# Mamba stage unrolled, with the recurrence of one batch beside the projections of the next

## The chip, the cores and the metric
The kernel is one program on one core of a Trainium2 chip. It runs eight stages one after the other (four attention-like and four feed-forward layers); the change is in the seventh, the Mamba layer. The metric is device microseconds of an execution. A core has TensorE (PE), VectorE (DVE), ScalarE (ACT), GpSimd (POOL) and SyncE (SP), each with its own instruction queue, which it works off in order; they wait for each other by semaphores. Matmuls write PSUM, which has eight banks of 128 x 512 fp32.

## The reference
Eight batches of 512 tokens with 256 channels go through all layers, each as `x + layernorm(layer(layernorm(x)))`. This is the Mamba layer, with 512 inner channels, 16 states, four taps and a step rank of 16:
```python
xr = x @ W_in.T
xc, res = (xr[..., :DI], xr[..., DI:])
u = depthwise_causal_conv(xc, W_conv)          # 4 taps a channel
u = silu(u + b_conv)
x_dbl = einsum('bdl,ed->ble', u, W_xproj)      # -> dt (16), B (16), C (16)
delta = softplus(dt @ W_dt.T + b_dt)
dA = exp(delta * A);  dBu = delta * B * u      # for each channel and state
h = dA_t * h + dBu_t                           # over the 512 tokens
y = sum_n(h * C) + u * D
out = (y * silu(res)) @ W_out.T
```

## The kernel before, in words
`stage_mamba` keeps channels on partitions: the 512 inner channels are four tiles (`ct`), tokens lie along the free dimension, 512 columns. After one block that loads weights and builds the selection table `sel`, a hardware loop `nc.Fori(0, NB)` runs the eight batches, one block each. Within a block the order of work is the order of the code of each engine:

- Projection: PE multiplies `w_in_t` with the normed, transposed rows (L1824), 8 tiles with K=256. ACT copies the first four to `xc` (L1779) and takes Silu of the others (`res`, L1781). VectorE convolves: four taps, 16 operations (L1704, L1707). ACT: Silu to `u_t` (L1785).
- PE projects `u_t` to 48 rows (L1829) and the step rows back to 512 channels (L1835). VectorE splits the B and C rows into three bf16 parts (L1716 to L1721), so that one bf16 matmul with `sel` can broadcast a row exactly over 128 partitions.
- Softplus: Abs, Exp, Ln on ACT (L1798, L1800, L1803), joined with a quadratic by three VectorE operations over all four tiles (L1729, L1731, L1732); then `delta` and `e_t = delta * u` (L1740).
- Recurrence: 64 units, state outside, tile inside. For each, ACT writes the decay exp(delta*A) to PSUM (L1812), VectorE makes dB (L1751) and scans over the tokens (L1762), POOL multiplies with the broadcast C (L1890), PE adds the product to the tile's sum in `pA` with an identity matmul (L1859). Per state, PE broadcasts C and B into the same bank (L1843, L1849) and ACT copies C out between them (L1795). Rings of three buffers.
- Norm of the next batch's rows is placed in the recurrence (L291 to L302, L138); output projection (L1873), then the output norm at the start of the next block (L151 to L179).

All eight PSUM banks are in use: `pA` four, `pX` two, `pY` two, which is at once decay and output.

## Time and profile before

| | |
|---|---|
| median of 3 runs | 6546.77 us (6545.3 to 6550.39) |
| profiled execution | 6538.69 us, span 6536.7 us |
| Mamba stage in the span | 4133.2 to 5577.6 us |
| busy over the span: PE, DVE, ACT, POOL | 68%, 47%, 29%, 29% |
| mean granted PE clock | 0.836 |

The busy shares are means over eight stages with different limits; the stage has to be read by itself. The granted clock is a share of 2.4 GHz, so 0.50 is the lower level, 1.2 GHz. In the timeline, a fp32 matmul of the code appears as two MATMUL instructions (two passes), and a group written "x4" has its start and its whole duration.

### The profile page before, as it was taken

To read this page: it belongs to the slowest core of one execution; us is meant where nothing else is said; L and a number is where in the kernel's file an instruction comes from. 1 tells how busy PE (TensorE), PEld (TensorE's weight loads), DVE (VectorE), ACT (ScalarE), POOL (GpSimd) and SP (SyncE) were. 2 spreads that over 40 slices of the span, in tenths; PEclk is the share of its full clock that TensorE was granted. 3 is DMA by queue.
4 is the path that set the end of the run, shared out by engine and by line. 5 is a ranking of instruction groups with operands and counts; after the bars stand their busy time and mean duration, and the time that the engine had idled before them with its cause. 6 is when DMAs were issued, how large, how long until landed. Compare 5 with 4: busy or idle time off the path is not lost. (4 is left out here: it accounts for less than half of the span.)

```text
span 6536.7 us, 62764 instructions
## 1 busy us (share of the span) xinstructions
PE 4465.0 (68%) x21090; PEld 2693.5 (41%) x21122; DVE 3088.5 (47%) x5209; ACT 1888.4 (29%) x3188; POOL 1907.6 (29%) x2039
## 2 busy tenths in 40 slices
PE   5696795588888288266666668566666666497772
PEld 2574673245555188144444434222222222354441
DVE  4514612244444733355555422488888888211113
ACT  3123222222222122243444312244444444011111
POOL 3522212222222055400100011355555555131112
PEclk8757857799999699588888889788899888599996
DMA  4711511200000489200000011100000000711113
GB/s 100 231 28 29 174 31 45 81 23 16 13 19 10 155 231 256 94 10 10 19 10 10 10 53 44 34 10 10 10 10 10 6 6 7 176 55 32 34 34 116
DMA packets 333314, 367.62 MB, mean 56 GB/s; under 512 B 70326, under 2 KB 283126, under 8 KB 332646
## 3 DMA queue, kind: packets, MB, share of 16 engines
q1 hardware_dynamic: 317462, 335.24, 17.0%
q0 software_dynamic: 15696, 30.33, 1.7%
q8 instruction: 95, 1.56, 0.1%
q14 instruction: 61, 0.50, 0.0%
HBM read 251.65 MB, written 113.84 MB: 56 GB/s over the span
## 5 line engine op out<-in xcount | busy, mean ns | idle before, releaser
L1859 PE MATMUL mamba_pA<-mamba_hC,ident 128*128 128x512 f32 x1024 | 613.9, 688 | 325.6 <-POOL mamba_hC L1890 323.8
L1890 POOL TENSOR_TENSOR mamba_hC<-mamba_h_t,mamba_cb 128x512 f32<-128x512 f32 x512 | 649.8, 1271 | 476.4 <-DVE mamba_h_t L1762 474.6
L1762 DVE TENSOR_TENSOR_SCAN mamba_h_t<-mamba_pY,mamba_dB 128x512 f32<-128x512 f32 x512 | 618.6, 1209 | 0.0
L1812 ACT ACTIVATE mamba_pY<-mamba_delta,mamba_a_neg 128x512 f32<-128x512 f32 x512 | 353.3, 691 | 471.8 <-DVE mamba_h_t L1762 438.6
L1859 PEld LDWEIGHTS mamba_pA<-mamba_hC,ident 128*128 128x128 f32 x1024 | 171.9, 204 | 717.2 <-POOL mamba_hC L1890 610.2
L1751 DVE TENSOR_TENSOR mamba_dB<-mamba_e_t,mamba_pX 128x512 f32<-128x512 f32 x512 | 335.4, 656 | 0.0
L709 DVE TENSOR_TENSOR top_x_in<-top_x_in,top_bank 128x512 f32<-128x512 f32 x71 | 48.8, 688 | 456.5 <-ACT top_x_in L772 456.5
L1192 POOL TENSOR_SCALAR mqa_prob<-mqa_prob,mqa_rinv 128x128 f32<-128x128 f32 (+3 forms) x256 | 136.9, 535 | 423.0 <-DVE mqa_rinv L1087 423.0
L866 PE MATMUL top_bank<-top_w,top_xgT 128*128 x568 | 255.6, 593 | 1.3 <-ACT top_xgT L754 1.2
L1399 DVE TENSOR_REDUCE mha_nmax<-mha_pS 128x4 f32<-128x512 f32 (+2 forms) x192 | 197.1, 1044 | 124.4 <-PE mha_pS L1501 123.2
L1460 ACT ACTIVATE mha_prob<-mha_pS 128x1024 f32<-128x1024 f32 (+1 forms) x192 | 167.6, 881 | 292.9 <-PE mha_pS L1519 292.4
L1119 ACT ACTIVATE mqa_prob<-mqa_pS,mqa_nmax 128x128 f32<-128x128 f32 (+3 forms) x256 | 134.9, 527 | 394.1 <-DVE mqa_nmax L1082 394.1
L934 POOL DMA_INDIRECT top_done<-top_y,top_xg x71 | 68.3, 962 | 555.9 <-ACT top_y L760 548.1
L128 POOL TENSOR_SCALAR mha_rstd<-mha_mv 128x4 f32<-128x4 f32 x9 | 2.1, 235 | 691.0 <-DVE mha_mv L117 691.0
L1082 DVE TENSOR_REDUCE mqa_nmax<-mqa_pS 128x1 f32<-128x128 f32 (+3 forms) x256 | 125.2, 489 | 161.7 <-PE mqa_pS L1150 161.1
L2253 PE MATMUL expert_pH<-expert_xgT,expert_w 128*128 128x128 f32 x1536 | 189.8, 282 | 0.0
L1148 PE MATMUL mqa_pS<-mqa_kT,mqa_qT 128*128 128x128 f32 (+3 forms) x512 | 181.6, 438 | 8.9 <-DVE mqa_v L1076 6.3
L2253 PEld LDWEIGHTS expert_pH<-expert_xgT,expert_w 128*128 128x128 f32 x1536 | 186.4, 198 | 0.0
L1167 PE MATMUL mqa_pO<-mqa_probT,mqa_v 128*128 128x512 f32 (+3 forms) x512 | 166.5, 471 | 6.3 <-DVE mqa_probT L1094 6.3
L1158 PE MATMUL mqa_pT<-ident,mqa_prob 128*128 128x128 f32 x640 | 120.1, 286 | 71.1 <-POOL mqa_prob L1192 70.6
L1389 DVE RECIPROCAL mha_rinv<-mha_pO 128x512 f32<-128x512 f32 x32 | 107.4, 3356 | 121.8 <-PE mha_pO L1540 121.8
L3211 PE MATMUL delta_bank<-delta_shared 128*128 128x128 f32 x1152 | 140.1, 282 | 34.6 <-DMA delta_shared<-delta_w 33.9
(566 smaller groups left out, 9942.5 us busy)
## 6 DMA issues: line engine op xcount, KB each, us to landing
expert_w<-in_L_ffn_W SPq DMA_DIRECT2D x48, 1024.0 KB, 5.9
delta_shared<-delta_w SPq DMA_DIRECT2D x64, 576.0 KB, 4.7
delta_w<-delta_wst SPq DMA_DIRECT2D x32, 576.0 KB, 2.8
expert_w<-in_L_ffn_W SPq DMA_DIRECT2D x48, 256.0 KB, 6.2
top_w<-in_L_ffn_w SPq DMA_DIRECT2D x24, 512.0 KB, 10.2
top_xg<-top_slots SPq DMA_DIRECT2D x71, 128.5 KB, 2.0
top_slots<-top_zrow SPq DMA_DIRECT2D x1, 9088.0 KB, 43.9
moe_sum<-expert_zero SPq DMA_DIRECT2D x16, 512.0 KB, 6.7
```

The source lines that it names most:

```text
L866: last = nc.tensor.matmul(bank[at + j % 2][:, :], xgT[:, j % 2, k * P:(k + 1) * P], wt[:, bass.ds(e * KD + k, 1), :].rearrange("p a h -> p ...
L1148: nc.tensor.matmul(pS[u % 2][:, 0:(q + 1) * P], qT[:, h, q * P:(q + 1) * P], kT[:, 0:(q + 1) * P], start=True, stop=False, skip_group_chec ...
L1167: last = nc.tensor.matmul(pO[h % 2][:, k * P:], v[:, k, :], probT[:, h % 2, k, k * P:], start=(k == 0), stop=(k == NT - 1), skip_group_che ...
L1399: nc.vector.tensor_reduce(nmax[:, i, h:h + m], by_unit(pS[j % BUF][:, :, :], m, (i + 1) * P), AX.X, ALU.max, negate=True).then_inc(max_rea ...
L1460: nc.scalar.activation(by_unit(prob[:, (weights - 1) % BUF, :, :], m, L - i * P), by_unit(pS[j % BUF][:, :, :], m, L - i * P), ACT.Exp).th ...
L1751: nc.vector.tensor_tensor(dB[:, u % 3, :], e_t[:, ct, :], pX[s % 2][:, :], ALU.mult)\
L1762: nc.vector.tensor_tensor_scan(h_t[:, u % 3, :], dA(u), dB[:, u % 3, :], 0.0, ALU.mult, ALU.add).then_inc(scan_ready, 1)
L1812: nc.scalar.activation(dA(u), delta[:, ct, :], ACT.Exp, scale=a_neg[:, ct, s:s + 1])\
L1859: nc.tensor.matmul(pA[:, ct, :], c.ident[:, :], hC[:, u % 3, :], start=(s == 0), stop=(s == NS - 1)).then_inc(sum_ps, 1)
L1890: nc.gpsimd.tensor_tensor(hC[:, u % 3, :], h_t[:, u % 3, :], cb[:, s % 3, :], ALU.mult)\
L2253: last = nc.tensor.matmul(pH[e % 2][:, s * MT + m, :], w1[:, e % WR, s, k, m::MT], xgT[:, e % 2, k, :], start=(k == 0), stop=(k == KD - 1))
L3211: last = nc.tensor.matmul(out, vp[:, n % 2, i, HB * (PAD - d):HB * (PAD - d) + P], wr[:, g % 3, at_col:at_col + P], start=(d == 0), stop=( ...
```

## The change
The stage becomes one block of straight code for all batches `a`; each has 64 units `u`. The unit number decides what else an engine does behind its own part of the unit: the projections of batch `a + 1`, the output of batch `a - 1`, the norm of `a + 2`. Helpers as `conv_in(a, ct)` hold one operation with its waits.

- The convolution is folded into the projection: at the start each half of W_in is multiplied with each tap (`w_taps`, four copies), and PE adds four shifted matmuls (K=256 each) in PSUM. VectorE's 16 operations and the copy to `xc` go; ACT adds the bias, and one Silu covers all four tiles.
- Units go by pairs of tiles: 16 states of tiles 0, 1, then of 2, 3. A state's B and C are broadcast once a pair, so twice in a batch. State sums need two banks (`pS`), decay has two (`pD`), broadcasts two (`pB`), and two (`pX`) are handed round for every projection result; `use(a, i)` numbers these uses, and a use waits for the copy-out of the one two before.
- Rings for dB, h, hC and cb have four buffers; u, res three batches; delta, e two.
- From VectorE to ACT: the bias of the step. To POOL: the square of the softplus (`square`) and `delta * u` (`step_times`).
- The first and last norm blocks and the block ends between batches go.

```diff
-    units = [(s, ct) for s in range(NS) for ct in range(CT)]
+    PAIR = 2
+    HALF = PAIR * NS
+    NU = CT // PAIR * HALF
+    PAD = CONV - 1
+    USES = 2 + 3 * CT + 1
+    RB, RC = 4, 4
...
-        pA = sc.ps("pA", [P, CT, L])
+        pS = [sc.ps(f"pS{k}", [P, L]) for k in range(PAIR)]
+        pD = [sc.ps(f"pD{k}", [P, L]) for k in range(2)]
+        pB = [sc.ps(f"pB{k}", [P, L]) for k in range(2)]
...
+        def use(a, i):
+            return USES * a + 2 * max(a - 2, 0) + i
+        def use_out(a):
+            return USES * min(a + 3, NB) + 2 * a
+        def unit(u):
+            return u // HALF, u % HALF // PAIR, u % PAIR
+        def tile_of(u):
+            return PAIR * (u // HALF) + u % PAIR
...
+                def state_in(n):
+                    a, u = n // NU, n % NU
+                    if u < PAIR or HALF <= u < HALF + PAIR:
+                        dve.wait_ge(z["e_ready"], CT * a + tile_of(u) + 1)
+                    if u % PAIR == 0:
+                        dve.wait_ge(z["b_ps"], n // PAIR + 1)
+                    if n >= RB:
+                        dve.wait_ge(z["scan_ready"], n - RB + 1)
+                    nc.vector.tensor_tensor(dB[:, n % RB, :], e_t[:, a % 2, tile_of(u), :], pB[n // PAIR % 2][:, :], ALU.mult)\
+                        .then_inc(z["db_ready"], 1)
...
+                for j in range(CONV):
+                    dve.wait_ge(z["tap_ps"], j + 1)
+                    for k in range(KD):
+                        last = nc.vector.tensor_tensor(w_taps[:, k, j, :], w_xc[:, k, :], pD[j % 2][:, :], ALU.mult)
+                    last.then_inc(z["tap_ready"], 1)
...
+                for a in range(NB):
+                    for u in range(NU):
+                        n = NU * a + u
+                        if n + 1 < NB * NU:
+                            state_in(n + 1)
+                        scan(n)
+                        if u == 1 and a:
+                            skip(2 * a - 1)
+                        elif u == HALF + 1:
+                            skip(2 * a)
+                        if a + 1 < NB:
+                            if u == 35:
+                                split_high(a + 1)
+                            elif u == 36:
+                                split_low(a + 1)
+                            elif u == 44:
+                                upper(a + 1)
+                            elif u == 51:
+                                lower(a + 1)
+                            elif u == 52:
+                                steps(a + 1)
+                        if u == 45 and a:
+                            out_stats(a - 1)
+                        if a + 2 < NB:
+                            if u == 56:
+                                stats(a + 2)
+                            elif u == 60:
+                                scale(a + 2)
...
+                def conv_in(a, ct):
+                    act.wait_ge(z["x_ps"], use(a, CONV_AT + ct) + 1)
+                    if a >= 3:
+                        act.wait_ge(z["y_ready"], CT * (a - 2))
+                    nc.scalar.activation(u_t[:, a % 3, ct, :], pX[use(a, CONV_AT + ct) % 2][:, :], ACT.Identity,
+                                         bias=b_conv[:, ct:ct + 1]).then_inc(z["x_free"], 1)
+                def silus(a):
+                    act.wait_ge(z["x_free"], use(a, CONV_AT + CT - 1) + 1)
+                    nc.scalar.activation(every(u_t[:, a % 3, :, :]), every(u_t[:, a % 3, :, :]), ACT.Silu)\
+                        .then_inc(z["u_ready"], 1)
+                    nc.scalar.activation(every(res[:, a % 3, :, :]), every(res[:, a % 3, :, :]), ACT.Silu)\
+                        .then_inc(z["z_ready"], 1)
...
+                def c_copy(r):
+                    act.wait_ge(z["c_ps"], r + 1)
+                    if r >= RC:
+                        act.wait_ge(z["hc_ready"], PAIR * (r - RC + 1))
+                    nc.scalar.activation(cb[:, r % RC, :], pB[r % 2][:, :], ACT.Copy).then_inc(z["c_ready"], 1)
+                def decayed(n):
+                    a, u = n // NU, n % NU
+                    g, s, i = unit(u)
+                    if u == 0:
+                        act.wait_ge(z["delta_ready"], a + 1)
+                    if n >= 2:
+                        act.wait_ge(z["scan_ready"], n - 1)
+                    ct = tile_of(u)
+                    nc.scalar.activation(pD[n % 2][:, :], delta[:, a % 2, ct, :], ACT.Exp, scale=a_neg[:, ct, s:s + 1])\
+                        .then_inc(z["da_ready"], 1)
...
+                for a in range(NB):
+                    for u in range(NU):
+                        n = NU * a + u
+                        decayed(n)
+                        if u % PAIR and (n + 3) // PAIR < NB * NU // PAIR:
+                            c_copy((n + 3) // PAIR)
+                        if a + 1 < NB:
+                            if u in (4, 5):
+                                turned(a + 1, u - 4)
+                            elif 6 <= u < 6 + CT:
+                                gate_in(a + 1, u - 6)
+                            elif u in (13, 17, 21, 25):
+                                conv_in(a + 1, (u - 13) // 4)
+                                if u == 25:
+                                    silus(a + 1)
+                            elif u == 32:
+                                xproj_in(a + 1)
+                            elif 34 <= u < 34 + CT:
+                                step_in(a + 1, u - 34)
+                            elif u == 38:
+                                decay_abs(a + 1)
+                            elif u == 40:
+                                decay_exp(a + 1)
+                            elif u == 42:
+                                log(a + 1)
+                        if u == 54 and a:
+                            out_rows(a - 1)
...
+                def gate(a, ct):
+                    out = into(use(a, Z_AT + ct))
+                    if ct == 0:
+                        pe.wait_ge(z["x_free"], use(a, T_AT + KD - 1) + 1)
...
+                def conv(a, ct, j):
+                    out = pX[use(a, CONV_AT + ct) % 2]
+                    if j == 0:
+                        into(use(a, CONV_AT + ct))
+                    for k in range(KD):
+                        last = nc.tensor.matmul(out[:, :], w_taps[:, k, j, ct * P:(ct + 1) * P], xnT[:, k, j:j + L],
+                                                start=(j == 0 and k == 0), stop=(j == CONV - 1 and k == KD - 1))
+                    if j == CONV - 1:
+                        last.then_inc(z["x_ps"], 1)
...
+                def broadcast_c(r):
+                    if r % HALF == 0:
+                        pe.wait_ge(z["parts_ready"], r // HALF + 1)
+                    if r >= 2:
+                        pe.wait_ge(z["db_ready"], PAIR * (r - 1))
+                    nc.tensor.matmul(pB[r % 2][:, :], sel[:, NS + r % NS, :], parts[:, r // HALF % 2, :], start=True, stop=True)\
+                        .then_inc(z["c_ps"], 1)
+                def broadcast_b(r):
+                    pe.wait_ge(z["c_ready"], r + 1)
+                    nc.tensor.matmul(pB[r % 2][:, :], sel[:, r % NS, :], parts[:, r // HALF % 2, :], start=True, stop=True)\
+                        .then_inc(z["b_ps"], 1)
...
+                for a in range(NB):
+                    for u in range(NU):
+                        n = NU * a + u
+                        add_state(n)
+                        r = n // PAIR + 3
+                        if r < NB * NU // PAIR:
+                            if n % PAIR == 0:
+                                broadcast_c(r)
+                            else:
+                                broadcast_b(r)
+                        if a + 1 < NB:
+                            if u < KD:
+                                turn(a + 1, u)
+                            elif u < KD + CT:
+                                gate(a + 1, u - KD)
+                            elif u < KD + CT + CT * CONV:
+                                i = u - KD - CT
+                                conv(a + 1, i // CONV, i % CONV)
+                            elif u in (28, 29):
+                                xproj(a + 1, u - 28)
+                            elif 31 <= u < 31 + CT:
+                                steps(a + 1, u - 31)
+                        if a and 37 <= u < 37 + CT:
+                            out(a - 1, u - 37)
...
+                for a in range(NB):
+                    for u in range(NU):
+                        state_out(NU * a + u)
+                        if u in (3, 4) and a:
+                            gated(2 * a - 1, u - 3)
+                        elif u in (HALF + 3, HALF + 4):
+                            gated(2 * a, u - HALF - 3)
+                        if a + 1 < NB:
+                            if 44 <= u < 44 + CT:
+                                square(a + 1, u - 44)
+                            elif 54 <= u < 54 + CT:
+                                step_times(a + 1, u - 54)
+                        if a:
+                            if u == 49:
+                                out_scale(a - 1)
+                            elif u in (59, 60):
+                                residual(a - 1, u - 59)
+                        if u == 58 and a + 2 < NB:
+                            variance(a + 2)
-        first_norm(nc, sc, n, src, c, pX, dch, lambda t: pY[:, t, :])
-        with nc.Fori(0, NB) as b:
...
-                    for j in range(CONV):
-                        for ct in range(CT):
-                            if j == 0:
-                                dve.wait_ge(xr_used, ct + 1)
-                                last = nc.vector.tensor_scalar(conv[:, ct, :], xc[:, ct, 0:L], w_conv[:, ct, 0:1], None,
-                                                               ALU.mult)
-                            else:
-                                last = nc.vector.scalar_tensor_tensor(conv[:, ct, :], xc[:, ct, j:j + L],
-                                                                      w_conv[:, ct, j:j + 1], conv[:, ct, :],
-                                                                      ALU.mult, ALU.add)
-                            if j == CONV - 1:
-                                last.then_inc(conv_ready, 1)
...
-        last_norm(nc, sc, n, src, dst, c, lambda t: pY[:, t, :], dch)
```

On PE, in the middle of the recurrence, three states before, and then two units of the convolution stretch after (`pS`, `pA`: state sums; `sel`: broadcasts; `w_taps`: folded convolution):
```order
L1859 MATMUL mamba_pA<-mamba_hC,ident 128x512 x3
L1843 MATMUL mamba_pX<-mamba_parts,mamba_sel 128x512
L1859 MATMUL mamba_pA<-mamba_hC,ident 128x512
L1849 MATMUL mamba_pX<-mamba_parts,mamba_sel 128x512
L1859 MATMUL mamba_pA<-mamba_hC,ident 128x512 x3
```
```order
L2060 MATMUL mamba_pS<-mamba_hC,ident 128x512
L2046 MATMUL mamba_pB<-mamba_parts,mamba_sel 128x512
L2018 MATMUL mamba_pX<-mamba_xnT,mamba_w_taps 128x512 x2
L2060 MATMUL mamba_pS<-mamba_hC,ident 128x512
L2051 MATMUL mamba_pB<-mamba_parts,mamba_sel 128x512
L2018 MATMUL mamba_pX<-mamba_xnT,mamba_w_taps 128x512 x2
```
Before, PE has a state sum per unit and two broadcasts per four units; now each unit also has a broadcast and two matmuls of a tap, 16 units in a row.

On ACT, from the x projection to the first decay before, and the end of the convolution stretch (units 23 to 27) after:
```order
L1788 ACTIVATE mamba_xdbl<-mamba_pX 48x512
L1798 ACTIVATE mamba_e_t<-mamba_delta 128x2048
L1800 ACT_TABLE_LOAD
L1800 ACTIVATE mamba_e_t<-mamba_e_t 128x2048
L1803 ACT_TABLE_LOAD
L1803 ACTIVATE mamba_conv<-mamba_e_t 128x2048
L1795 ACTIVATE mamba_cb<-mamba_pX 128x512 x2
L1812 ACT_TABLE_LOAD
```
```order
L1920 ACTIVATE mamba_cb<-mamba_pB 128x512
L1930 ACTIVATE mamba_pD<-mamba_delta,mamba_a_neg 128x512 x2
L1920 ACTIVATE mamba_cb<-mamba_pB 128x512
L1876 ACTIVATE mamba_u_t<-mamba_pX,mamba_b_conv 128x512
L1881 ACT_TABLE_LOAD
L1881 ACTIVATE mamba_u_t<-mamba_u_t 128x2048
L1883 ACTIVATE mamba_res<-mamba_res 128x2048
L1930 ACT_TABLE_LOAD
L1930 ACTIVATE mamba_pD<-mamba_delta,mamba_a_neg 128x512 x2
```
Silu, with a table load on each side, now stands between the decay of unit 25 and that of unit 26, and the C copy of unit 25 ahead of it.

## Rows read from the trace of the kernel before

**Rows 1.** The page, its first line: span and instructions of the execution.
```profile
span 6536.7 us, 62764 instructions
```

**Rows 2.** Windows of one batch, its two long parts; columns as the view's head.
```profile
core 0: us, PE busy (x) PEld busy (x) DVE busy (x) ACT busy (x) POOL busy (x), PEclk, DMA share, GB/s
4342.50:4390.50 48.00, 24.66 (x52) 9.21 (x52) 30.88 (x47) 22.77 (x28) 5.51 (x8) 0.76 0.10 33
4390.50:4502.90 112.40, 82.04 (x160) 25.33 (x160) 112.36 (x139) 51.81 (x78) 80.89 (x65) 0.91 0.00 0
```

**Rows 3.** Timeline in the steady recurrence; start, duration, engine, line, operation, wait before.
```profile
4451.03 1.21 DVE L1762 TENSOR_TENSOR_SCAN mamba_h_t<-mamba_pY,mamba_dB 128x512 f32<-128x512 f32 x1
...
4451.93 1.12 PE L1859 MATMUL mamba_pA<-mamba_hC,ident 128*128 128x512 f32 x2 [0.59 <-POOL mamba_hC L1890]
...
4452.27 0.69 ACT L1812 ACTIVATE mamba_pY<-mamba_delta,mamba_a_neg 128x512 f32<-128x512 f32 x1 [1.02 <-DVE mamba_h_t L1762]
4452.31 1.27 POOL L1890 TENSOR_TENSOR mamba_hC<-mamba_h_t,mamba_cb 128x512 f32<-128x512 f32 x1 [0.44 <-DVE mamba_h_t L1762]
4452.74 1.21 DVE L1762 TENSOR_TENSOR_SCAN mamba_h_t<-mamba_pY,mamba_dB 128x512 f32<-128x512 f32 x1
```

**Rows 4.** Groups by line and shape, VectorE, the stage; count, busy, mean ns, idle before.
```profile
L1771 DVE SCALAR_TENSOR_TENSOR mamba_u_t<-mamba_u_t,mamba_d_skip,mamba_pA 128x512 f32<-128x512 f32 x32 | 22.9, 735 | 5.1 <-PE mamba_pA L1859 5.0
...
L1729 DVE SCALAR_TENSOR_TENSOR mamba_quad<-mamba_e_t 128x2048 f32<-128x2048 f32 x8 | 18.3, 2293 | 41.6 <-ACT mamba_e_t L1800 41.6
...
L1717 DVE TENSOR_TENSOR mamba_rest<-mamba_xdbl,mamba_parts 32x512 f32<-32x512 f32 x8 | 5.4, 679 | 0.3
```

**Rows 5.** The same view, GpSimd, whole span: a scaling over 512 columns.
```profile
L1192 POOL TENSOR_SCALAR mqa_prob<-mqa_prob,mqa_rinv 128x512 f32<-128x512 f32 x64 | 44.5, 695 | 22.5 <-DVE mqa_rinv L1087 22.5
```

**Rows 6.** Timeline of ScalarE in the projection.
```profile
4347.94 0.60 ACT L1779 ACTIVATE mamba_xc<-mamba_pA 128x512 f32<-128x512 f32 x1 [1.57 <-PE mamba_pA L1824]
4349.65 0.60 ACT L1779 ACTIVATE mamba_xc<-mamba_pA 128x512 f32<-128x512 f32 x1 [1.12 <-PE mamba_pA L1824]
```

**Rows 7.** Timeline of PE: broadcast and sum in a row, then the output matmuls.
```profile
4398.35 0.38 PE L1849 MATMUL mamba_pX<-mamba_parts,mamba_sel 96*128 96x512 bf16 x1
4398.57 1.02 PE L1859 MATMUL mamba_pA<-mamba_hC,ident 128*128 128x512 f32 x2
...
4505.84 7.14 PE L1873 MATMUL mamba_pY<-mamba_w_out,mamba_res 128*128 128x256 f32 x32 [0.19 <-POOL mamba_res L1899]
```

**Rows 8.** Timeline of ScalarE in the softplus.
```profile
4371.44 1.91 ACT L1798 ACTIVATE mamba_e_t<-mamba_delta 128x2048 f32<-128x2048 f32 x1 [5.86 <-DVE mamba_delta L1725]
4373.37 1.28 ACT L1800 ACT_TABLE_LOAD   x1
4374.66 1.91 ACT L1800 ACTIVATE mamba_e_t<-mamba_e_t 128x2048 f32<-128x2048 f32 x1
```

**Rows 9.** Windows for the granted clock (PEclk), columns as in rows 2.
```profile
3812.00:3832.00 20.00, 20.00 (x63) 11.64 (x62) 2.75 (x4) 2.02 (x4) 0.00 (x0) 1.00 0.00 0
...
4548.00:4572.00 24.00, 3.40 (x6) 0.91 (x5) 17.73 (x19) 13.23 (x12) 2.54 (x2) 0.50 0.00 0
...
4588.00:4595.00 7.00, 6.46 (x9) 2.11 (x8) 7.00 (x10) 3.52 (x6) 6.39 (x7) 0.56 0.00 0
...
4615.00:4672.00 57.00, 41.77 (x85) 12.00 (x84) 57.00 (x68) 27.62 (x42) 42.00 (x34) 0.99 0.00 0
```

**Rows 10.** Timeline where the stage begins and ends.
```profile
4133.18 0.37 SPq L1652 DMA_DIRECT2D mamba_w_in_t<-in_L_attn_W_in  x1
...
4138.60 11.61 POOL L1678 TENSOR_SCALAR_AFFINE_SELECT mamba_sel<-mamba_sel 32x4096 bf16<-32x4096 bf16 x3
...
4216.54 1.22 DVE L1762 TENSOR_TENSOR_SCAN mamba_h_t<-mamba_pY,mamba_dB 128x512 f32<-128x512 f32 x1
...
5549.38 2.32 DVE L1762 TENSOR_TENSOR_SCAN mamba_h_t<-mamba_pY,mamba_dB 128x512 f32<-128x512 f32 x2
...
5577.61 0.37 SPq L591 DMA_DIRECT2D top_wr<-in_L_ffn_w_router  x1
```

More of the change, by code:

```diff
@@ new lines, in out_rows @@
+                def out_rows(a):
+                    act.wait_ge(z["y_scale"], 3 * (a + 1))
+                    if a:
+                        act.wait_ge(y_st, 16 * a)
+                    for t in range(NT):
+                        last = nc.scalar.activation(yn[:, t, :], pX[(use_out(a) + t // 2) % 2][:, t % 2 * D:(t % 2 + 1) * D],
+                                                    ACT.Identity, bias=ynm[:, t:t + 1], scale=yrstd[:, t:t + 1])
+                        if t % 2:
+                            last.then_inc(z["x_free"], 1)
@@ new lines, in _ @@
+                act.wait_ge(z["w_in"], 16 * 11)
+                nc.scalar.activation(every(a_neg), every(a_neg), ACT.Exp).then_inc(z["a_exp"], 1)
+                for k in range(KD):
+                    turned(0, k)
+                for ct in range(CT):
+                    gate_in(0, ct)
+                for ct in range(CT):
+                    conv_in(0, ct)
+                silus(0)
+                xproj_in(0)
+                for ct in range(CT):
+                    step_in(0, ct)
+                decay_abs(0)
@@ new lines, in residual @@
+                def residual(a, half):
+                    pool.wait_ge(z["x_free"], use_out(a) + half + 1)
+                    pool.wait_ge(xr_in[a % 2], 16 * (a // 2 + 1))
+                    part = slice(2 * half, 2 * half + 2)
+                    last = nc.gpsimd.tensor_tensor(yn[:, part, :], yn[:, part, :], xr[:, a % 2, part, :], ALU.add)
+                    if half:
+                        last.then_inc(z["y_out"], 1)
+                variance(0)
+                variance(1)
+                pool.wait_ge(z["a_exp"], 1)
@@ new lines, in _ @@
+                nc.gpsimd.tensor_scalar(every(a_neg), every(a_neg), -1.0, None, ALU.mult).then_inc(z["pz"], 1)
+                for ct in range(CT):
+                    square(0, ct)
+                for ct in range(CT):
+                    step_times(0, ct)
+                for a in range(NB):
+                    for u in range(NU):
[9 more added lines that the diff above has]
+                                step_times(a + 1, u - 54)
+                        if a:
+                            if u == 49:
[4 more added lines that the diff above has]
+                            variance(a + 2)
@@ L1905, in stage_expert_choice @@
+                for i in range(PAIR):
+                    gated(2 * NB - 1, i)
+                out_scale(NB - 1)
+                residual(NB - 1, 0)
+                residual(NB - 1, 1)
+        sc.clear()
 def stage_expert_choice(nc, w, src, dst, c):
```

549 lines of the change are left out of this document (323 added, 226 removed).

## The prediction

> **What bounds the kernel now.** I read the page first for the size of the whole [rows 1], then the windows of one batch, the timeline inside it, the groups by line, and last the clock windows. The stage runs from its first load at 4133.2 to the next stage's first at 5577.6 [rows 10]: 1444.4 us of the 6536.7. The windows cut a batch in two [rows 2]. For 112.4 us VectorE is busy 112.36: the recurrence, bound by VectorE alone. For 48.0 us before that it is busy 30.9: projections, convolution and softplus wait for each other in a row. Then 13.4 us of output projection and block ends, so 173.8 us per batch.
> In the steady recurrence the scans start every 1.71 us (4451.03, 4452.74) [rows 3]. Call scan, dB product, decay, hC product and state sum of one of the 64 (tile, state) pairs a unit. POOL needs 1.27 of the 1.71, ACT 0.69 plus 0.60 for a C copy now and then, PE two passes for the sum. All but VectorE have slack, and that is where the change puts the next batch's projections.
>
> **What a unit costs PE.** An fp32 matmul of 512 columns is two passes. In the projection a tile with K=256 (two matmuls) is drained every 1.71 us (4347.94, 4349.65) [rows 6], so one such matmul costs 0.856. A broadcast (bf16) costs 0.22: 4398.35 to 4398.57 [rows 7]. Four output matmuls of 256 columns are 8 of 32 passes that took 7.14, so 1.78 [rows 7]. After the change a unit has one state sum and one broadcast (pairs of tiles double the broadcasts): 1.07. Added to it:
> - units 0, 1: four transposes each, some 0.55
> - units 2 to 5: one gate tile, 1.71
> - units 6 to 21: one tap of the folded convolution, two matmuls, 1.71. The convolution leaves VectorE, but the x half of the projection grows from 8 to 32 matmuls
> - units 28, 29: 1.71; 31 to 34: 0.86; 37 to 40: 1.78 (output of the batch before).
> Over 64 units that is 117 us, near VectorE's, but it stands in a lump: in units 2 to 21 PE needs 1.07+1.71 = 2.78 us against 1.71. This lump is the step on which the forecast rests.
>
> **The lump, step by step** (0 is the end of a full batch's scan 0). Scans 0, 1, then two skip products of 0.74 [rows 4], scan 2 at 4.9. ACT turns the second half of x at its unit 5, behind the decay (6.6+0.7) and a C copy (to 8.0), ready at 8.7; the first gate matmul needs both halves. From there PE has 1.71 and 19 units of 2.78: the last tap ends at 63.2. VectorE cannot run ahead: dB of unit 2r needs broadcast r, which PE issues at unit 2r-5, and ACT's gate and conv copies at unit u wait for PE's unit u-4 with the decay of u+1 behind them in ACT's queue. So scan 25 ends near 63, where free running would have 26x1.71+1.5 = 46 for scan 26.
> Then Silu: the C copy of unit 25 needs the broadcast behind the last tap (+1.7), conv copy 0.6, table load 1.28, two Silus over 2048 columns at 1.91 each, table load 1.28, decay 0.69 [rows 3, 8]; scan 26 follows it and ends at 63.2+10.6 = 73.8. That is 27.8 us of stall per batch. The wait here is ACT's, and who waits for it is the scan: two decay banks cover only some 1.5 us.
> Rest of the batch: 38 scans, 65.0. Vector extras: skip 1.5; six conversions over 32 partitions of at most 0.68 each, 3.1 together; three operations of 2048 columns at 2.29, 6.9 [rows 4]; statistics and scaling of a later batch 3.5 (now 112.4 against 63x1.71+1.21 in [rows 2, 3]); output statistics half of that, 1.8: 16.8. Smaller stalls: x projection in units 28, 29 (copy waits some 7 us behind scan 28) 1.0; Ln with its two table loads 2.4 (1.28+1.91+1.28+0.69 against the slack); scaling waits for POOL's rstd 0.9. Batch: 73.8+65.0+16.8+4.3 = 159.9.
> Moved to POOL at no price: squares (tensor_scalar 0.70 [rows 5] and a product 1.27, four times) in units 44 to 47 are 8.1 us beyond 5.1 of hC, against 6.9 of scans with 2.29+1.8 vector work beside; POOL falls back 2 to 3 us, and a broadcast has about 3 us of room. If that room is gone it costs up to 3 us a batch. POOL's other products (units 54 to 60) fall back 1 to 3 us in the same way. SP only loads and stores rows, three times 0.5 MB a batch, a transfer queue that nothing in the recurrence waits for.
> Clock: cold stretches in units 26 to 55, see below; 2 us taken, bounds 0 and 7: 162 per batch.
>
> **Start and end.** The first batch's projection has nothing to lie beside. PE waits for POOL's selection tables (now 4138.60+11.61, 17 us after the start [rows 10]); then tap weights (four broadcasts and eight products, in VectorE's queue ahead of the norm) to 26, norm and transposes to 34.5, four gate tiles with a cold start to 44, 32 tap matmuls 27.4 to 71.5, Silu, x projection and step matmuls to 84.5, Abs, Exp, Ln with two loads (3x1.91+2x1.28 [rows 8]) to 93, squares on POOL to 98, three vector operations to 102.6, products, first scan's end at 105.8. Today it is at 4217.8 (4216.54+1.22 [rows 10]), so 84.6 after the start: 21 us worse, once. At the end the last scan to the next stage's start is now 25.9 (5549.38+2.32 = 5551.7 to 5577.6 [rows 10]); the separate norm block goes, 19.5.
>
> **Sum.** 105.8 + first batch 158.7 (no skip nor output statistics) + 5x162 + batch 6 157.6 (no later rows to norm) + last batch without projections 63x1.71+3.0+1.8 = 112.5 + 19.5 = 1364. Against 1444.4 that is 80 us less. The profiled execution took 6538.7 with a span of 6536.7 [rows 1], so 6458; the median of the runs is 8 above it, so 6467.
>
> **Two rules and their rows.** Clock: PE fully busy with 512 columns held the full 2.4 GHz for 20 us (3812 to 3832, 1.00); after 24 us with PE busy 3.4 it was at 1.2 GHz (0.50); in the recurrence that follows it fell again to 0.56 for 7 us near 4588, and then held 0.99 for 57 us at 42 busy [rows 9]. So the lump should run at full clock, and the dips should come after the Silu stall. The Trainium skill (TensorE: Matmul & The Clock Gate, What's actually happening) says that half rate is the resting state and activity lifts it; by that rule, with which these rows agree, the lump keeps itself fast.
> Table switches: load at 4373.37, 0.02 behind the Abs, Exp 0.01 behind the load [rows 8], so I price a switch at 1.28. The Trainium skill (ScalarE: Activation LUTs, What ACT_TABLE_LOAD costs) adds a drain of 1380 ns to each; no row here shows it. By that page four switches inside the recurrence would cost 5.5 more a batch, an estimate, and the time would be 6505.
>
> **Rivals.**
> A. As above, 6467; its own range 6430 to 6500. Chance 0.66.
> B. The lump hides (PE units take less than 2.78, or the vector engine is far enough ahead): minus 27.8 and the clock's 2 to 4, seven times: 6245. Against it: the 1.71 per tile is throughput of a busy PE. Halves of it are as likely as the whole. 0.09.
> C. Slower: PE enters the lump from a 60% busy stretch at 1.2 GHz and stays there part of the way. The lump is 55.6 us at full clock; it eats the whole gain of 80/7 = 11.5 per batch when its mean grant is 0.83 or less; at 0.75 it takes 74.1, 7x18.5 = 130 more: 6597. For it: the 0.50 and 0.56 rows; against it: 1.00 under full load. 0.08.
> D. The handoffs between PE, ACT and VectorE in the lump do not overlap as I have them and a unit is longer: at 3.1 us 6512, at 3.3 us 6540, no gain. This is also the case in which the change does not do what it says, overlap. 0.12.
> E. Each table switch costs as much again as its load: 4x1.28x7 = 36 more: 6503. 0.05.
>
> **Numbers.** Predicted 6467. The range goes from 6415 (A with no small stalls and no dips, and a little of B) to 6540 (D, E): 8 in 10. A measurement tells 0.2%, 13 us, from no change. Faster by more: A, B, E and half of D, 0.84; within: part of D and of C, 0.06; slower: C and the rest of D, 0.10.
>
> **What would show it.** In the profile after: the stage near 1364 us; first scan's end 106 us after the first load; scans 1.71 apart in units 26 to 63 but 2.78 apart on average in 5 to 25, with PE busy without a gap there and the clock at 1.00; one gap of 7 to 9 us between scans 25 and 26 that ACT's Silu ends; full batches 162 us apart. It is wrong if PE has gaps in units 2 to 21, if the clock there is under 0.9, if the distance of scans there stays near 1.71, or if POOL is what scans or broadcasts wait for in units 44 to 60.

## The result and the profile after

The changed kernel took 6578.8 us (median of 6 runs, 6564.5 to 6585.4); the kernel before 6546.2. The ratio is 1.0048, with a 95% interval of 1.0035 to 1.0061: slower by half a per cent, where 6467 was predicted and 6540 was the end of the range. The profiled execution took 6575.4.

The page's first line, which answers to [rows 1]:

```profile
span 6573.7 us, 63859 instructions
```

The stage went from 1444.4 us (its ends in [rows 10]) to 1477.4; the prediction had 1364. By the scans, one after the other: the first ends 115.4 after the start (predicted 105.8), the batches take 172.4, 174.8, 176.8, 174.8, 176.8, 174.8 and 170.3 (predicted 158.7, five of 162, 157.6), the last 117.4 (112.5), the tail 23.9 (19.5). Of the 113 us missed 94 lie in the seven batches with projections beside them, 9.6 in the start, 4.9 in the last batch and 4.4 in the tail.

First the lump. Windows of batch 3, from the start of its first scan (4777.3) to scan 26, and from there to the next batch; columns as in [rows 2]:

```profile
4777.30:4852.00 74.70, 66.89 (x171) 28.91 (x169) 47.56 (x56) 35.29 (x54) 36.21 (x29) 0.98 0.00 1
4852.00:4952.10 100.10, 77.67 (x158) 28.41 (x159) 90.63 (x107) 48.39 (x72) 77.61 (x60) 0.76 0.05 15
```

and ScalarE's timeline around scan 26, with the scan from VectorE's:

```profile
4843.49 0.60 ACT L1920 ACTIVATE mamba_cb<-mamba_pB 128x512 f32<-128x512 f32 x1 [3.80 <-PE mamba_pB L2046]
4843.99 0.68 ACT L1876 ACTIVATE mamba_u_t<-mamba_pX,mamba_b_conv 128x512 f32<-128x512 f32 x1
4844.69 1.28 ACT L1881 ACT_TABLE_LOAD   x1
4845.98 1.91 ACT L1881 ACTIVATE mamba_u_t<-mamba_u_t 128x2048 f32<-128x2048 f32 x1
4847.80 1.89 ACT L1883 ACTIVATE mamba_res<-mamba_res 128x2048 f32<-128x2048 f32 x1
4849.71 1.28 ACT L1930 ACT_TABLE_LOAD   x1
```
```profile
4851.73 1.22 DVE L1786 TENSOR_TENSOR_SCAN mamba_h_t<-mamba_pD,mamba_dB 128x512 f32<-128x512 f32 x1 [8.63 <-ACT mamba_pD L1930]
```

Scan 26 ends 74.4 us after scan 0 (predicted 73.8), behind one wait of 8.63; TensorE's clock there is 0.98. Between scans 5 and 25 a unit takes 2.70 on average (predicted 2.78). The lump is as forecast. The second window is not: 100.1 us, where the 38 scans need 65.0 (1.71 each) and the prediction had 88.1 with extras, small stalls and clock.

What fills it stands in the groups by line over the stage (count, busy, mean ns, idle before):

```profile
L1738 DVE TENSOR_SCALAR mamba_xn<-mamba_x,mamba_mv,mamba_rstd 128x256 f32<-128x256 f32 x32 | 31.9, 1056 | 4.3 <-POOL mamba_rstd L2147 3.7
L1767 DVE SCALAR_TENSOR_TENSOR mamba_delta<-mamba_delta,mamba_ln 128x2048 f32<-128x2048 f32 x8 | 25.2, 3147 | 0.0
L1762 DVE SCALAR_TENSOR_TENSOR mamba_ln<-mamba_e_t,mamba_ln 128x2048 f32<-128x2048 f32 x8 | 23.7, 2968 | 6.8 <-POOL mamba_e_t L2157 6.8
...
L1757 DVE TENSOR_TENSOR mamba_ln<-mamba_ln,mamba_decay 128x2048 f32<-128x2048 f32 x8 | 18.3, 2283 | 12.0 <-ACT mamba_ln L1914 12.0
L1752 DVE TENSOR_TENSOR mamba_rest<-mamba_rest,mamba_mid 32x512 f32<-32x512 f32 x8 | 12.2, 1530 | 0.1
...
L2154 POOL TENSOR_SCALAR mamba_e_t<-mamba_decay 128x512 f32<-128x512 f32 x32 | 47.7, 1491 | 58.5 <-ACT mamba_decay L1908 58.5
```

The subtraction of 32 partitions took 679 ns in [rows 4] and takes 1530 on average (680 in the first batch, where GpSimd stands still, 1650 in the others). Of the operations of 2048 columns, 2293 before, the step (L1767) takes 3147 on average and the maximum with the quadratic (L1762) 2968; the minimum (L1757) keeps 2283. The first half of a square was priced 695 by [rows 5] and takes 1491. The waits of 6.8 in L1762's row and of 12.0 in L1757's lie in the start alone; later batches have none there. The scan (1215) and the skip (729) are as they were. And ScalarE waits longer and longer for the broadcast of C, with decays queued behind the copy (its timeline, the copies of units 45, 47 and 49; waits of 6.25 and 4.57 follow in units 51 and 53):

```profile
4897.18 0.60 ACT L1920 ACTIVATE mamba_cb<-mamba_pB 128x512 f32<-128x512 f32 x1 [1.11 <-PE mamba_pB L2046]
...
4903.97 0.60 ACT L1920 ACTIVATE mamba_cb<-mamba_pB 128x512 f32<-128x512 f32 x1 [2.28 <-PE mamba_pB L2046]
...
4911.03 0.60 ACT L1920 ACTIVATE mamba_cb<-mamba_pB 128x512 f32<-128x512 f32 x1 [4.19 <-PE mamba_pB L2046]
```

Behind the broadcast stands GpSimd. Its timeline from unit 43 on (a state product, then per unit the two halves of a square and the next state product), and the window of these units:

```profile
4897.13 3.23 POOL L2173 TENSOR_TENSOR mamba_hC<-mamba_h_t,mamba_cb 128x512 f32<-128x512 f32 x1 [0.44 <-DVE mamba_h_t L1786]
4900.33 1.49 POOL L2154 TENSOR_SCALAR mamba_e_t<-mamba_decay 128x512 f32<-128x512 f32 x1
4901.91 1.27 POOL L2157 TENSOR_TENSOR mamba_e_t<-mamba_e_t,mamba_decay 128x512 f32<-128x512 f32 x1
4903.13 1.26 POOL L2173 TENSOR_TENSOR mamba_hC<-mamba_h_t,mamba_cb 128x512 f32<-128x512 f32 x1
4904.36 1.50 POOL L2154 TENSOR_SCALAR mamba_e_t<-mamba_decay 128x512 f32<-128x512 f32 x1
```
```profile
4902.00:4927.00 25.00, 16.08 (x20) 4.63 (x21) 21.22 (x24) 7.02 (x13) 24.53 (x19) 0.50 0.00 1
```

GpSimd needs 4.03 a unit there against 1.71, and is busy 24.5 of 25. TensorE's sum waits for its product and the broadcast of C stands behind the sum. The clock is 0.50 in this window, so a sum takes 2.08 instead of 1.02. TensorE still waits 0.5 to 1.5 for GpSimd before each of four sums in a row, so GpSimd sets the pace; what the low clock adds behind it was not separated.

From the end of scan 48 to that of scan 53 it takes 18.9 us, where the prediction's terms give 13.2; from scan 32 to 37, with the split, 18.9 instead of 14.1.

### The profile page after: what moved, and what is told of

It is laid out like the page before. It is cut to its first block and busy times, and to the rows that moved or that the text cites. A ratio compares the mean times of both kernels' runs of the same rounds, so it can differ in the third digit from the quotient of the medians.

```text
span 6573.7 us, 63859 instructions
## 1 busy us (share of the span) xinstructions
PE 4720.6 (72%) x21766; PEld 2827.0 (43%) x21766; DVE 3007.7 (46%) x4971; ACT 1958.9 (30%) x3326; POOL 2058.7 (31%) x2110
## 5 line engine op out<-in xcount | busy, mean ns | idle before, releaser
L2173 POOL TENSOR_TENSOR mamba_hC<-mamba_h_t,mamba_cb 128x512 f32<-128x512 f32 x512 | 678.3, 1330 | 457.6 <-DVE mamba_h_t L1786 448.2
L2060 PE MATMUL mamba_pS<-mamba_hC,ident 128*128 128x512 f32 x1024 | 652.3, 724 | 137.0 <-POOL mamba_hC L2173 128.9
L1786 DVE TENSOR_TENSOR_SCAN mamba_h_t<-mamba_pD,mamba_dB 128x512 f32<-128x512 f32 x512 | 622.0, 1215 | 237.2 <-ACT mamba_pD L1930 237.1
L1930 ACT ACTIVATE mamba_pD<-mamba_delta,mamba_a_neg 128x512 f32<-128x512 f32 x512 | 345.3, 688 | 143.0 <-DVE mamba_h_t L1786 126.7
L2060 PEld LDWEIGHTS mamba_pS<-mamba_hC,ident 128*128 128x128 f32 x1024 | 204.4, 221 | 422.8 <-POOL mamba_hC L2173 307.5
L1778 DVE TENSOR_TENSOR mamba_dB<-mamba_e_t,mamba_pB 128x512 f32<-128x512 f32 x512 | 339.9, 664 | 32.3 <-PE mamba_pB L2051 29.7
L1920 ACT ACTIVATE mamba_cb<-mamba_pB 128x512 f32<-128x512 f32 x256 | 152.4, 596 | 497.9 <-PE mamba_pB L2046 494.1
L2018 PE MATMUL mamba_pX<-mamba_xnT,mamba_w_taps 128*128 128x512 f32 x512 | 238.2, 591 | 0.0
L1517 PE MATMUL mha_pS<-mha_qkT 128*128 128x256 bf16 (+3 forms) x512 | 147.6, 357 | 39.6 <-ACT mha_qkT L1451 28.3
```

What stands on the lines that cost most here:

```text
L1778: nc.vector.tensor_tensor(dB[:, n % RB, :], e_t[:, a % 2, tile_of(u), :], pB[n // PAIR % 2][:, :], ALU.mult)\
L1786: nc.vector.tensor_tensor_scan(h_t[:, n % RB, :], pD[n % 2][:, :], dB[:, n % RB, :], 0.0, ALU.mult, ALU.add).then_inc(z["scan_ready"], 1)
L1930: nc.scalar.activation(pD[n % 2][:, :], delta[:, a % 2, ct, :], ACT.Exp, scale=a_neg[:, ct, s:s + 1])\
L2018: last = nc.tensor.matmul(out[:, :], w_taps[:, k, j, ct * P:(ct + 1) * P], xnT[:, k, j:j + L], start=(j == 0 and k == 0), stop=(j == CONV ...
L2060: nc.tensor.matmul(pS[i][:, :], c.ident[:, :], hC[:, n % RB, :], start=(s == 0), stop=(s == NS - 1))\
L2173: nc.gpsimd.tensor_tensor(hC[:, n % RB, :], h_t[:, n % RB, :], cb[:, r % RC, :], ALU.mult)\
```

## The experiments

Theory 1: VectorE's operations with two inputs in SBUF, its conversions and scalings, and GpSimd's operations exclude each other, and GpSimd falls back behind them. Theory 2: GpSimd is merely overloaded. "Stage" is from its first load to the next stage's (1444.4 before), "start" to the end of the first scan, "batch" that of batch 3; these three are of one profiled execution each. The chips differ: beside e5, e6 and e7 the kernel before took 6595.7 us, beside e9 6601.6, and elsewhere 6546 to 6548. So the ratio is what compares, and for these four runs a time is the ratio times 6546.

| kernel | ratio to before, 95% | stage | start | batch |
|---|---|---|---|---|
| changed | 1.0048 (1.0035 to 1.0061) | 1477.4 | 115.4 | 174.8 |
| e1 one tap | 0.9835 (0.9819 to 0.9851) | 1334.0 | 94.8 | 159.6 |
| e2 squares, products on VectorE | 1.0017 (1.0007 to 1.0026) | 1460.1 | 108.9 | 174.4 |
| e3 no square | 0.9973 (0.9963 to 0.9983) | 1431.9 | 107.4 | 170.6 |
| e5 norm in the stall | 1.0001 (0.9991 to 1.001) | 1448.5 | 115.4 | 170.4 |
| e6 and square on VectorE | 0.9958 (0.9943 to 0.9973) | 1421.8 | 108.4 | 167.3 |
| e7 lump flattened | 0.9841 (0.9828 to 0.9855) | 1337.7 | 101.6 | 155.5 |
| e9 later rows | 0.9818 (0.9803 to 0.9833) | 1326.5 | 100.5 | 157.0 |
| e11 square in two-operation form | 1.0006 (0.9996 to 1.0015) | 1453.6 | 111.9 | 171.4 |

**e1, one tap.**
```diff
-                    for k in range(KD):
-                        last = nc.tensor.matmul(...)
                     if j == CONV - 1:
+                        for k in range(KD):
+                            last = nc.tensor.matmul(...)
```


> Part of the computation is left out: of the four taps of the folded convolution only the last is multiplied, 8 matmuls a batch instead of 32. Theory 1 (the lump on TensorE is as forecast; the missing time lies in the vector operations and GpSimd after unit 32): 24 matmuls of 0.856 go, 20.5 us a batch, scan 26 ends about 54 us after scan 0 instead of 74.4, eight batches give 6415 (6400 to 6440), and the stretch from scan 32 to 61 stays at 85 us. Rival (another stage or ScalarE's chain sets the pace of units 2 to 25): scan 26 moves by less than 5 us and the time stays above 6540.

Measured 6439.3, the upper end. Scan 26 ends at 57.0, not 54, and the batches are 15 to 20 us shorter. Scans 32 to 61 take 86.9 us (84.9 in the changed kernel): the lump's price is TensorE's, and the loss behind it does not depend on it.

**e2, squares and products back to VectorE.**
```diff
+    nc.vector.scalar_tensor_tensor(every(e_t[:, a % 2, :, :]), every(decay), -2.0, every(decay), ALU.add, ALU.mult)
...
-    elif 54 <= u < 54 + CT:
-        step_times(a + 1, u - 54)
```


> The squares (one operation of 2048 columns at unit 43) and the products of step and input (four at unit 54) go back from GpSimd to VectorE. Theory 1 (the missing 13.5 us a batch are VectorE and GpSimd excluding each other, and GpSimd falling back behind it): the waits for the C copy after scan 48 go (6 us), but VectorE gains 2.3 to 3.2 plus four times 0.7 to 1.5; the batch comes to 174 to 177 and the time to 6560 to 6590. Theory 2 (GpSimd is merely overloaded by the moved work, VectorE's prices are as stand-alone): all 13.5 us go and 5 come, batch 166, time 6515.

6558.7, by the time just outside theory 1's range on its good side and far from 6515. Scans 48 to 53 come down to 14.1 us; VectorE's four products take 944 ns on average, because in each batch one of the four takes 1.75 and the others 0.68.

**e3, no square.**
```diff
-    dve.wait_ge(z["quad_ready"], CT * (a + 1))
...
-    if 44 <= u < 44 + CT:
-        square(a + 1, u - 44)
```


> Part of the computation is left out: the squares; the bound of the logarithm is taken from the decay itself. GpSimd has 11 us less a batch in units 44 to 47, nothing is added elsewhere. Theory 1 (exclusion of two-input VectorE operations and GpSimd): the 6 us of late C copies between scans 48 and 53 go, the stretched vector operations stay: scan 32 to 37 still 18.8, scan 57 to 61 still 12; batch 168, time 6525 (6515 to 6540). Theory 2 (overload): 13 us a batch go, time 6480, and the split operations come down to 0.4 to 0.7 us.

6527.6, as theory 1 had it; theory 2's 6480 falls. The batch, forecast at 168, takes 170.5. So 5.3 us of a batch (175.8, the mean of 174.8 and 176.8, to 170.5) were the squares'; some 1.1 of them is the step's operation, which no longer meets a busy GpSimd (3.36 to 2.27). The split is untouched; the groups by line, as above:

```profile
L1752 DVE TENSOR_TENSOR mamba_rest<-mamba_rest,mamba_mid 32x512 f32<-32x512 f32 x8 | 12.2, 1530 | 0.1
```

**e4 and e8, pairs of operations by themselves.**
```diff
+        for f, nf in ((scan, N), (tt_psum, N), (tt_sbuf, N), (tt_32, N), (cast_32, N), (ts_256, N), (stt_2048, 3), ...):
+            phase(f, None, nf)
+            phase(f, prod, nf)
```


> The disputed cost by itself: the eight stages are left out, and the output is a copy of the input. Ten kinds of VectorE operation run in a row, each first alone, then with GpSimd multiplying 128x512 tiles from the on-chip memory, then with GpSimd adding a constant to such tiles. Theory 1: operations with two inputs in the on-chip memory, casts and tensor_scalar lengthen beside GpSimd (0.4 to 0.7 us becomes 1.3 to 1.6; 2.3 becomes 3 or more) and GpSimd's product goes from 1.27 to 2 or more beside them; operations with one input in the accumulation memory (scan, dB product, skip) stay within 5 per cent of their time alone. Theory 2: nothing lengthens by more than 10 per cent on either engine.

> Again the disputed costs by themselves: the eight stages are left out and the output is a copy of the input. First GpSimd alone: a product of two tiles of 128x512, then a constant added, a constant multiplied, and a column value (one for each partition) multiplied and added. If the price 0.70 of the prediction holds only for a column value, the constants take 1.49 and the columns 0.70; if it holds for a product only, both additions take 1.49. Then VectorE beside GpSimd: the conversion and the subtraction of the split and a scaling, each reading the accumulation memory. Theory 1 (turns are taken only where VectorE reads two inputs, or converts or scales, in the on-chip memory): within 5 per cent of their time alone beside the product; the rival (any VectorE operation but a scan or product waits) gives 1.4 to 1.8. A minimum of 2048 columns beside products: 3.4, as 2.29 plus one turn of 1.09, where four of 512 columns pay four turns (7.1).

VectorE's timeline of e4 (start, duration of the row's operations together): for each kind alone, then beside GpSimd's products.

```profile
38.63 9.03 DVE L3861 TENSOR_TENSOR_SCAN pair_o<-pair_ps,pair_b 128x512 f32<-128x512 f32 x8 [31.83 <-PEq L3897]
47.96 9.03 DVE L3861 TENSOR_TENSOR_SCAN pair_o<-pair_ps,pair_b 128x512 f32<-128x512 f32 x8 [0.30 <-PEq L3897]
...
97.88 4.91 DVE L3867 TENSOR_TENSOR pair_o<-pair_a,pair_b 128x512 f32<-128x512 f32 x8 [7.12 <-PEq L3897]
103.09 13.73 DVE L3867 TENSOR_TENSOR pair_o<-pair_a,pair_b 128x512 f32<-128x512 f32 x8 [0.30 <-PEq L3897]
...
162.14 2.76 DVE L3873 CAST pair_obf<-pair_a 32x512 bf16<-32x512 f32 x8 [6.49 <-PEq L3897]
165.21 11.40 DVE L3873 CAST pair_obf<-pair_a 32x512 bf16<-32x512 f32 x8 [0.30 <-PEq L3897]
...
215.95 6.70 DVE L3879 SCALAR_TENSOR_TENSOR pair_o<-pair_a,pair_b 128x2048 f32<-128x2048 f32 x3 [8.07 <-PEq L3897]
222.95 10.01 DVE L3879 SCALAR_TENSOR_TENSOR pair_o<-pair_a,pair_b 128x2048 f32<-128x2048 f32 x3 [0.30 <-PEq L3897]
```

Per operation: 0.68 to 1.78, conversion 0.41 to 1.47, scaling of 256 columns 0.41 to 1.38, 2048 columns 2.29 to 3.38. Each time it is some 1.0 to 1.1 us more, whatever the operation's length, a little less than GpSimd's product takes (1.26): one turn. GpSimd's own product takes 1.75 beside the two-input operations of 512 columns, where 2 or more was expected, 1.33 to 1.47 beside scaling and conversion, and 3.35 beside the long ones. Beside GpSimd's additions of a constant (1.49) the turn costs less: every second product of VectorE takes 1.09, the others 0.68. Scan, dB product, skip and statistics take the same time beside GpSimd as alone. In e8 the conversion that reads PSUM is slower alone but takes no turns (VectorE's timeline, alone and beside products), and a minimum of 2048 columns goes from 2.29 to 3.38:

```profile
75.82 4.86 DVE L3906 CAST pair_obf<-pair_ps 32x512 bf16<-32x512 f32 x8 [69.02 <-PEq L3918]
80.99 4.87 DVE L3906 CAST pair_obf<-pair_ps 32x512 bf16<-32x512 f32 x8 [0.30 <-PEq L3918]
```

Theory 1's mechanism holds in both runs. On GpSimd's additions e8's first guess fell: constant or column, all forms took 1.49 to 1.57, and 0.70 stayed unexplained until e10.

**e5, the norm in the stall.**
```diff
-    if u == 56: stats(a + 2)
-    elif u == 60: scale(a + 2)
...
+    if u == 25: stats(a + 2)     # scale(a + 2) ahead of scan 26
```


> Only the place of the norm changes: statistics and the four scalings of batch a+2 move from units 56 and 60 into unit 25, where VectorE waits 8.6 us for the Silus and GpSimd has nothing to multiply. Theory 1 (two-input operations, casts and tensor_scalar take turns with GpSimd, about 1.09 us more for each): scans 53 to 61 lose 2.5 + 5.2 us, the stall takes them, the batch comes from 175 to 168 in six batches, time 6535 (6525 to 6548). Theory 2 (each costs what it costs alone): 3.5 + 0.9 us go a batch, time 6552.

The same line in the groups by line, now with GpSimd idle beside it:

```profile
L1738 DVE TENSOR_SCALAR mamba_xn<-mamba_x,mamba_mv,mamba_rstd 128x256 f32<-128x256 f32 x32 | 11.1, 408 | 8.4 <-POOL mamba_rstd L2146 8.4
```

From 1056 ns to 408: the mechanism inside the kernel. Scans 53 to 61 take 15.1 instead of 21.5, and the gap before scan 26 stays 10.4, so the stall hides what moved there. The time alone does not decide: 1.0001 times 6546 is 6547, at the edge of theory 1's range and nearer to theory 2's 6552 than to 6535. The stage fell by 29 us, not 42: the seven batches gave 34, since behind unit 60 a wait of 0.6 to 1.9 us for a late broadcast shows, which the scalings had covered, and the last batch grew by 2.7 and the tail by 2.3, whose cause stays open.

**e6, and the squares on VectorE.** The edit of e5 and e2's square at unit 43.

> As the run before, and the squares go from GpSimd (two operations of 1.49 for each of four tiles) to one VectorE operation of 2048 columns at unit 43; the products of step and input stay on GpSimd. Theory 1: the 6 us of late C copies go, 2.3 to 3.4 come, so about 3 us a batch less than the run before: 6512 (6500 to 6525). Theory 2: 8 to 9 us a batch less, 6475.

The stage fell by 27 us from e5: 7 at the start, and batches by 1.1 to 3.4, as theory 1 has it and not theory 2's 8 to 9; 0.9958 of 6546 is 6519.

**e7, the lump flattened.**
```diff
-    elif u < KD + CT:
-        gate(a + 1, u - KD)
-    elif u < KD + CT + CT * CONV: ...
+    elif u < 26:
+        for i in range((u - 2) * 4 // 3, (u - 1) * 4 // 3):
+            conv(a + 1, i)                       # one matmul each
...
+    elif 39 <= u < 39 + CT * KD:
+        gate(a + 1, (u - 39) // KD, (u - 39) % KD)
```


> As the run before, and TensorE's lump is flattened: the gate tiles leave units 2 to 5 for units 39 to 46 (one matmul a unit, their Silu a batch later, at the next stall), and the 32 tap matmuls spread over units 2 to 25 (four in three units) instead of 6 to 21. With the lump as forecast (2.78 a unit for 20 units), a unit now takes 1.07 + 1.14 = 2.2, scan 30 comes 7 us earlier, a batch takes about 161 to 163, and the first batch's projection is 12 us shorter: 6450 (6430 to 6480), faster than both kernels. Rival (the stall for Silu and the handoffs, not the rate of TensorE, set the pace, so spreading only moves the wait): 6495 to 6510.

0.9841 times 6546 is 6442: expected 6450. The parts came out otherwise than the sum: the batches take 151 to 159, not 161 to 163, and the start is 7 us shorter, not 12. Scan 30 ends at 71.7 instead of 81.2; this is the lump's part, and 7 us were expected. The run changes more than the lump: split and softplus moved to other units, and some of them no longer wait for a turn (one conversion 1.37 to 0.41, the maximum with the quadratic 3.25 to 2.26), which was not tested by itself. Its windows of batch 3, before and after scan 30's start:

```profile
4707.70:4779.40 71.70, 65.20 (x167) 28.07 (x167) 56.87 (x76) 36.56 (x56) 44.03 (x37) 0.97 0.07 22
4779.40:4863.20 83.80, 67.19 (x161) 26.51 (x161) 75.76 (x89) 47.24 (x70) 59.73 (x45) 0.90 0.00 1
```

Up to the scan behind the Silus (30 here, 26 in the changed kernel) VectorE is busy 57 of 72 us, where it was 48 of 75.

**e9, later rows.** GpSimd's products at units 53, 55, 57, 59, its scale at 58, the rows at 61.

> The flattened version again, and GpSimd's extra work at the end of a batch is thinned: the four products of step and input in units 53, 55, 57, 59 instead of 54 to 57, the scale of the output rows at 58 instead of 55, and ScalarE's rows at 61. In the flattened version scans 59 to 61 lose 3 to 4 us a batch because ScalarE waits 2.8 for that scale with decays behind it. If that wait is the cause, 3 us a batch, ratio to the kernel before 0.981; if GpSimd's total in units 53 to 63 is what is late (12 us of products beside 19 us of scans), the loss only moves and the ratio stays at 0.984.

0.9818; the stage is 11 us shorter than e7's, the intervals just overlap. Scans 58 to 61 are now 1.7 apart (3.85 and 2.44 in e7), but the three behind them take 7.8 us instead of 5.4: most of the loss moved. The seven batches together gave 6 of the 11 us, not 3 each; 4 came in the tail, which was not forecast. This is the fastest version, 1.8% faster than the kernel before, but whether it beats e7 the times do not show.

**e10 and e11, the form of the square.**
```diff
-    nc.gpsimd.tensor_scalar(e_t[...], decay[:, ct, :], -2.0, None, ALU.add)
+    nc.gpsimd.tensor_scalar(e_t[...], decay[:, ct, :], -2.0, 1.0, ALU.add, ALU.mult)
```


> GpSimd alone, the eight stages left out and the output a copy of the input: tensor_scalar over 128x512 with one operation (constant added, nothing second) took 1.49 and with a column 1.56, while the row behind the price 0.70 of the prediction multiplies by a column and then by 1.0, in place. If the second operation makes it fast, two_ops and two_ops_column take 0.70 out of place too; if writing in place does, only the in-place forms do. Beside VectorE's two-input products: if the turn is held only by the part of an operation that reads or writes, the fast form adds less than 1.09 to them, at most 0.7.

> The changed kernel with one edit: the first half of each square on GpSimd is written with a second operation (times 1.0), nothing else. If that form takes 0.70 instead of 1.49, GpSimd has 3.2 us a batch less in units 44 to 47, it falls back less, the late C copies after scan 48 shrink by 3 us a batch and the start by 3.2: 6555 where the changed kernel takes 6579, ratio to the kernel before 1.001. If the late copies are not due to GpSimd's squares, or the form is no faster, the ratio stays 1.005.

GpSimd's groups of e10, alone (L3894 one operation, L3900 column and times 1.0, L3903 and L3906 in place, one and two operations):

```profile
L3903 POOL TENSOR_SCALAR pair_po<-pair_po 128x512 f32<-128x512 f32 x8 | 11.7, 1490 | 0.3 <-DVEq L3909 0.3
L3894 POOL TENSOR_SCALAR pair_po<-pair_pa 128x512 f32<-128x512 f32 x8 | 11.7, 1490 | 0.4 <-PEq L3909 0.4
...
L3900 POOL TENSOR_SCALAR pair_po<-pair_pa,pair_pb 128x512 f32<-128x512 f32 x8 | 5.4, 695 | 0.3 <-PEq L3909 0.3
L3906 POOL TENSOR_SCALAR pair_po<-pair_po 128x512 f32<-128x512 f32 x8 | 4.7, 620 | 0.3 <-DVEq L3909 0.3
```

A second operation makes it 0.62 to 0.70; beside this form VectorE's products of two inputs take 1.09 instead of 1.78. In the kernel (e11) the line takes

```profile
L2154 POOL TENSOR_SCALAR mamba_e_t<-mamba_decay 128x512 f32<-128x512 f32 x32 | 21.9, 684 | 58.0 <-ACT mamba_decay L1908 57.5
```

and the batch, the start and the time fall by 3.4, 3.5 and 27 us, as expected (6551.3).

## Why the prediction was wrong

- **The lump** was right in each part: 2.78 a unit (2.70 measured), the stall of Silu, scan 26 within 0.6 us, table switches at their load alone (1.28, and 0.02 to the next operation). Rivals A and B were rightly ordered; C's half clock did not come where TensorE is full.
- **The vector extras, 16.8 us a batch,** are the term that failed. In the second window of batch 3 VectorE is busy 90.6 us, where scans and extras were to be 65.0 + 16.8 = 81.8, so the extras took 25.6. It is idle 9.5, where small stalls and clock were to be 4.3 + 2. These two, 8.8 and 3.2 us, and 0.6 before scan 26 are the 12.8 by which this batch missed 162. The extras grew because GpSimd multiplies states all the time: four operations of the split, up to two of 2048 columns and the four scalings each wait for a turn of it. The split and the long operations were priced at durations from a stretch in which GpSimd stood still: 3.8 and 1.8 us too little. The scalings were priced in the old recurrence, where GpSimd has gaps of 0.44 [rows 3]. There the trace before already shows the turn: in each batch one of the four scalings took 1.36 us and the others 0.40, which the mean hides (in batch 1 the slow one starts at 4427.96, and GpSimd's product had started at 4427.81). Now it is all four in most batches, 2.9 us more. Its line in the groups of the kernel before:

```profile
L302 DVE TENSOR_SCALAR mamba_xn<-mamba_x,mamba_mv,mamba_rstd 128x256 f32<-128x256 f32 x32 | 18.5, 636 | 0.0
```

- **"Moved to POOL at no price"** was the second. The prediction gave 3 us of room and named the loss if it went. It went: the squares take 2.8 each, not 2.0, because [rows 5] showed a form with a second operation (3.2 us a batch, e11), and GpSimd's product beside a long VectorE operation takes 3.2 to 3.4. Without squares the batch is 5.3 shorter (e3), more than the 3 named.
- **Clock:** the 2 us taken for cold stretches behind the Silu can't be judged. The clock was 0.76 in the second window, and no run varied it alone.
- **Start and end:** 9.6 and 4.4 us. The squares' form is 3.5 of the start (e11). The step matmuls end 87.9 after the start, where 84.5 was forecast, at a clock of 0.67 to 0.68 behind the taps; this and the rest of the start were read, not tested. In the last batch VectorE is busy 112.45, as forecast (112.5); the 4.9 more are idle time, nearly all in units 41 to 46. There ScalarE's C copies wait 4.35 and 3.82 for broadcasts behind the output matmuls of units 37 to 40, which with sum and broadcast come 2.80 apart on TensorE against 1.71: a second, small lump that the prediction had not priced (read, not tested). Why the tail is longer stays open.
- No rival had this mechanism: of the signs named, only "POOL is what scans or broadcasts wait for in units 44 to 60" came, by way of the sum on TensorE, as the C copies and GpSimd's window show.
- Two slips of the arithmetic decided nothing: four squares at 0.70 and 1.27 make 7.9, not 8.1, and the chances of A, B, E and half of D add to 0.86, not 0.84.

The Trainium skill (SBUF — State Buffer, Who interferes with whom) states the rule that was not weighed: VectorE operations with two inputs in SBUF contend with a GpSimd operation that reads it, as can copies, casts and tensor_scalar, and the one that comes second blocks for the whole instruction. e4 and e8 agree, with 1.09 us for a turn of a product that takes 1.26. So does the minimum of 2048 columns in the changed kernel: it starts 0.16 us ahead of GpSimd's product and keeps its 2.27, and the product takes the 3.23 shown above.

## What to carry to other kernels

A duration is a price only together with what runs beside it, and a mean can hide one slow operation among fast ones, so look at the single durations. Before moving VectorE or GpSimd work under a recurrence, ask of each operation whether it reads two tiles in SBUF, converts or scales, and whether GpSimd works there; such operations belong into gaps in which it stands still. A lump of TensorE work should be spread over as many units as the data's due time allows, since a full lump of 2.78 against 1.71 costs the difference in every unit. And a row of the profile prices an operation only in the same form.

## What the runs showed of the hardware

- Beside a dense stream of GpSimd's products the exchange of turns cost about one product for each VectorE operation, independent of its length: each of three of 2048 columns paid 1.09, each of eight of 512 columns 1.09 to 1.10 (e4). Beside GpSimd's one-operation addition it was 0.41 on every second one (e4), beside its two-operation form 0.41 on nearly each (e10).
- Who starts first does not pay: the same minimum of 2048 columns took 3.38 beside running products (e8) and 2.27 in the changed kernel, where GpSimd's product paid.
- GpSimd's tensor_scalar over 128x512 took 1.49 with one operation and 0.62 with two, in place or not (e10). Why one operation takes longer than two stays open.
- A conversion of 32x512 took 0.41 from SBUF and 0.67 from PSUM alone, but 1.47 and 0.67 beside GpSimd's products (e4, e8).
